# Conditional MLP with layer norm: fewer warm-up matmuls and a halved first cast at the start, the last batch's first tile's statistics on ScalarE at the end

## What is computed

```python
out_nr  = gelu(x @ w1_nr  + b1_nr)  @ w2_nr  + b2_nr
out_tsr = gelu(x @ w1_tsr + b1_tsr) @ w2_tsr + b2_tsr
h       = gelu(x @ w1_sr  + b1_sr)                      # 1024 wide
out_sr  = gelu(h @ w2_sr  + b2_sr)  @ w3_sr  + b3_sr
y   = x + where(c == 0, out_nr, where(c == 1, out_tsr, where(c == 2, out_sr, 0)))
mu  = mean(y); var = mean((y - mu) ** 2)                # over the 512 features
out = (y - mu) * rsqrt(var + 1e-5) * gamma + beta
```

## Time and profile before

| | us |
|---|---|
| median of 3 runs (lowest to highest) | 559.64 (559.57 to 559.65) |
| the profiled execution, its own time | 559.41 |
| span of the profiled execution, first to last instruction | 557.7 |
| TensorE busy | 549.6, 99% of the span |
| VectorE, ScalarE, GpSimd busy | 273.9, 213.5, 248.3 |

### The profile page before, as it was taken

The page is one execution under the profiler, slowest core; times in us unless marked ns, Lnnn a source line. Parts: engine busy times, 40 slices in busy tenths (PEclk is TensorE's granted clock), DMA queues, the critical chain, the costliest instruction groups (busy, mean ns, idle before and its releaser), DMA issues. The chain is left out here.

```text
span 557.7 us, 8222 instructions
## 1 busy us (share of the span) xinstructions
PE 549.6 (99%) x2423; PEld 453.4 (81%) x2424; DVE 273.9 (49%) x448; ACT 213.5 (38%) x328; POOL 248.3 (45%) x196
## 2 busy tenths in 40 slices
PE   9999999999999999999999999999999999999994
PEld 6888888888888888888888888888888888888883
DVE  5660176775856956114710569112765105601657
ACT  5451336145244354214421452424255124513351
POOL 0979898765674575300430046600174300430056
PEclk9999999999999999999999999999999999999998
DMA  8876405245344444200320044400244100410032
GB/s 313 339 237 190 152 7 196 100 151 188 109 155 145 156 150 141 84 0 0 138 87 0 1 158 142 150 0 0 75 150 159 66 0 29 154 43 0 0 135 91
DMA packets 26370, 61.28 MB, mean 110 GB/s; under 512 B 3058, under 2 KB 3314, under 8 KB 26226
## 3 DMA queue, kind: packets, MB, share of 16 engines
q1 hardware_dynamic: 26208, 60.97, 31.9%
q10 hardware_dynamic: 146, 0.13, 0.1%
HBM read 44.31 MB, written 16.78 MB: 110 GB/s over the span
## 5 line engine op out<-in xcount | busy, mean ns | idle before, releaser
L467 DVE TENSOR_TENSOR g_lo<-bank,g_hi 128x512 fp32r<-128x512 f32 x112 | 77.5, 692 | 251.0 <-DVEq L117 250.9
L415 ACT ACTIVATE g_hi<-bank,bcol 128x512 fp32r<-128x512 f32 x112 | 77.9, 695 | 165.9 <-ACTq L117 164.7
L620 POOL TENSOR_TENSOR rstd<-var_eps,power 128x2 f32<-128x2 f32 x30 | 21.0, 699 | 239.7 <-POOLq L117 239.7
L616 POOL TENSOR_TENSOR y<-y,row 128x512 f32<-128x512 f32 x64 | 95.7, 1514 | 49.1 <-POOLq L117 48.9
L437 ACT ACTIVATE y<-y,rstd 128x512 f32<-128x512 f32 x63 | 42.3, 717 | 166.3 <-ACTq L117 166.3
L244 PE MATMUL bank<-w_hi,g_hi 128*128 128x512 f32 x256 | 99.6, 389 | 0.0
L245 PE MATMUL bank<-w_lo,g_hi 128*128 128x512 f32 x256 | 99.6, 389 | 0.0
L246 PE MATMUL bank<-w_hi,g_lo 128*128 128x512 f32 x256 | 99.6, 389 | 0.0
L244 PE MATMUL bank<-x_hi,w_hi 128*128 128x512 f32 x240 | 93.4, 389 | 0.0
L245 PE MATMUL bank<-x_lo,w_hi 128*128 128x512 f32 x240 | 93.4, 389 | 0.0
L246 PE MATMUL bank<-x_hi,w_lo 128*128 128x512 f32 x240 | 93.4, 389 | 0.0
(11 more groups left out here) (42 smaller groups left out, 580.2 us busy)
## 6 DMA issues: line engine op xcount, KB each, us to landing
y<-x SPq DMA_DIRECT2D x64, 256.0 KB, 3.6
out<-y SPq DMA_DIRECT2D x63, 256.0 KB, 2.5
stage<-x_t SPq DMA_DIRECT2D x31, 512.0 KB, 3.3
w_raw<-weights SPq DMA_DIRECT2D x17, 512.0 KB, 5.1
row<-rows SPq DMA_DIRECT2D x1, 1280.0 KB, 11.0
stage<-x_t SPq DMA_DIRECT2D x2, 256.0 KB, 3.2
w_raw<-weights SPq DMA_DIRECT2D x2, 256.0 KB, 4.0
out<-y SPq DMA_DIRECT2D x1, 128.0 KB, 1.9
```

The costliest lines, as they stand in the source:

```text
L415: eng.activation(g_hi[:, slot, :], psum, ACT.Gelu, bias=b)
L467: eng.tensor_tensor(g_lo[:, slot, :], psum, g_hi32[:, slot, :], ALU.subtract).then_inc(s_gs, 1)
L616: eng.tensor_tensor(y[:, t, :], y[:, t, :], row[:, kind, :], ALU.add).then_inc(s_xb, 1)
L620: eng.tensor_tensor(rstd[:, t:t + n], var_eps[:, t:t + n], power[:, t:t + n], ALU.pow).then_inc(s_rstd, n)
```

## The change

At the start, 7 short matmuls on the constant are issued in place of 14. VectorE casts `w_hi` of chunks 0 and 1 in two halves of 256 columns, each raising `s_first_w`, and TensorE waits for the first half before `j` = 0 and for the second before `j` = 2. GpSimd sets one more small tile, `eps`.

In all batches but the last, epsilon is added for tiles 0 and 1 by GpSimd, inside `deviations(0, 2)`, and no longer by VectorE; for tiles 2 and 3 VectorE still does it.

In the last batch, ScalarE makes the statistics of tile 0, behind its last gelu: a copy of bank 4 with the sum of each row (`total`), the mean with minus sign, the mean into `mv`, the sum of squares of the deviations (`squares`), and the variance with epsilon. VectorE drops `bn_stats`, `bn_aggr` and `variance` of tile 0, waits for ScalarE before `centre` of tile 0, and does `variance` of tile 1 before `residual` of tile 2.

```diff
--- before.py
+++ after.py
@@ -38,7 +38,7 @@
 FINISHED_BY_OTHERS_END = TT - 1
 
 
-N_WARM, N_WARM_SHORT = 9, 14
+N_WARM, N_WARM_SHORT = 9, 7
 
 
 def conditional_mlp(nc, x, x_t, cond, weights, bias_cols, rows, out):
@@ -73,6 +73,8 @@
         rstd = sb("rstd", [P, TT])
         power = sb("power", [P, TT])
         unused = sb("unused", [1, 1])
+
+        total, minus_mean, squares, eps = sb("total", [P, 1]), sb("minus_mean", [P, 1]), sb("squares", [P, 1]), sb("eps", [P, 1])
         bank = [ctx.enter_context(nc.psum_tensor(f"bank{i}", [P, 512], fp32)) for i in range(8)]
 
         g_hi32 = g_hi[:, :, :].bitcast(fp32)
@@ -104,9 +106,11 @@
         s_y, s_acc = sem("s_y"), sem("s_acc")
         s_row = [sem(f"s_x_row{t}") for t in range(TT)]
         s_xb, s_ev, s_bn, s_mv = sem("s_xb"), sem("s_ev"), sem("s_bn"), sem("s_mv")
-        s_var = sem("s_var")
+        s_moments, s_eps, s_var = sem("s_moments"), sem("s_eps"), sem("s_var")
         s_own = sem("s_own")
         s_rstd, s_rstd_end = sem("s_rstd"), sem("s_rstd_end")
+        s_made, s_total, s_mean, s_squares, s_stats0, s_var0 = [
+            sem(n) for n in ("s_made", "s_total", "s_mean", "s_squares", "s_stats0", "s_var0")]
         s_v, s_v_end = sem("s_v"), sem("s_v_end")
         s_n = sem("s_n")
         s_fin, s_fin_end = sem("s_fin"), [sem(f"s_fin_end{h}") for h in range(2)]
@@ -287,7 +291,6 @@
                     take(eng, s_x01, 1)
                     for c in range(2):
                         eng.wait_ge(s_first, c + 1)
-                        eng.wait_ge(s_first_w, c + 1)
                         for which in range(3):
                             if which == 1:
                                 if c == 0:
@@ -298,6 +301,8 @@
                             if which == 2:
                                 eng.wait_ge(s_nr, 2 + c)
                             for j in range(HC):
+                                if which == 0 and j % 2 == 0:
+                                    eng.wait_ge(s_first_w, 2 * c + j // 2 + 1)
                                 part(j, c, which)
                         if c == 0:
                             read_next()
@@ -419,6 +424,20 @@
                 take(eng, s_full[f], 16)
                 eng.copy(x_hi[:, 2 * f:2 * f + 2, :], stage[:, f, :, :]).then_inc(s_hi, 1)
 
+            def first_tile_statistics(kind):
+
+                made = y[:, 0, :] if kind == NONE else bank[4][:, :]
+                take(eng, s_made)
+                eng.activation(bank[0][:, :], made, ACT.Copy, accum_out=total[:, :]).then_inc(s_total, 1)
+                take(eng, s_total)
+                eng.activation(minus_mean[:, :], total[:, :], ACT.Copy, scale=-1.0 / H).then_inc(s_mean, 1)
+                eng.activation(mv[:, 0, 0:1], total[:, :], ACT.Copy, scale=1.0 / H)
+                take(eng, s_mean)
+                eng.activation(bank[0][:, :], made, ACT.Square, bias=minus_mean[:, :], accum_out=squares[:, :]).then_inc(s_squares, 1)
+                take(eng, s_squares)
+                eng.sem_inc(s_stats0, 1)
+                eng.activation(var_eps[:, 0:1], squares[:, :], ACT.Identity, scale=1.0 / H, bias=eps[:, :]).then_inc(s_var0, 1)
+
             def body(kind, read_next, last):
                 for j in range(n_hidden(kind)):
                     gelu(bank[hidden_bank(kind, j)][:, :], j % 4, B1[kind] + j)
@@ -426,7 +445,9 @@
                 if kind == SR:
                     for i in range(HC):
                         gelu(bank[i][:, :], i, B2[SR] + i, (1, 1, 2, 0)[i])
-                if not last:
+                if last:
+                    first_tile_statistics(kind)
+                else:
                     split_x(0)
                     split_x(1)
                 for t in range(FINISHED_BY_OTHERS_END if last else TT):
@@ -475,11 +496,13 @@
             def made_in(kind, t):
                 return y[:, t, :] if kind == NONE else bank[4 + t][:, :]
 
-            def residual(kind, t):
+            def residual(kind, t, done=s_ev):
                 take(eng, s_xb)
                 if kind != NONE:
                     take(eng, s_y)
-                    eng.tensor_tensor(bank[4 + t][:, :], bank[4 + t][:, :], y[:, t, :], ALU.add).then_inc(s_ev, 1)
+                    eng.tensor_tensor(bank[4 + t][:, :], bank[4 + t][:, :], y[:, t, :], ALU.add).then_inc(done, 1)
+                elif done is s_made:
+                    eng.sem_inc(s_made, 1)
 
             def stats(kind, t):
                 if kind != NONE:
@@ -525,22 +548,24 @@
                     stats(kind, t + 1)
                     moments(kind, t)
                     moments(kind, t + 1)
-                    variance(t, 2)
+                    if t == 0:
+                        take(eng, s_mv, 2)
+                        eng.sem_inc(s_moments, 2)
+                    else:
+                        variance(t, 2)
                     centre(kind, t)
                     centre(kind, t + 1)
 
             def body_end(kind, read_next):
                 hidden(kind)
-                residual(kind, 0)
-                stats(kind, 0)
+                residual(kind, 0, s_made)
                 residual(kind, 1)
-                moments(kind, 0)
                 stats(kind, 1)
-                variance(0)
+                take(eng, s_stats0)
                 centre(kind, 0)
                 moments(kind, 1)
+                variance(1)
                 residual(kind, 2)
-                variance(1)
                 centre(kind, 1)
                 stats(kind, 2)
                 moments(kind, 2)
@@ -567,9 +592,10 @@
 
             for c in range(2):
                 eng.wait_ge(s_w_piece[c], 16)
-                eng.tensor_copy(w_hi[:, c, :], w_raw[:, c, :]).then_inc(s_first_w, 1)
+                for half in (slice(0, H // 2), slice(H // 2, H)):
+                    eng.tensor_copy(w_hi[:, c, half], w_raw[:, c, half]).then_inc(s_first_w, 1)
                 x_low(c, c + 1, (s_nr, s_x01)[c])
-                eng.wait_ge(s_first_w, c + 1)
+                eng.wait_ge(s_first_w, 2 * c + 2)
                 w_low(c, 0)
             x_low(2, 3, s_nr)
             x_low(3, 4, s_x23)
@@ -616,11 +642,17 @@
                         eng.tensor_tensor(y[:, t, :], y[:, t, :], row[:, kind, :], ALU.add).then_inc(s_xb, 1)
 
             def deviations(t, n):
-                take(eng, s_var, n)
+
+                if t == 0:
+                    take(eng, s_moments, n)
+                    eng.tensor_scalar(var_eps[:, t:t + n], mv[:, t:t + n, 1], EPS, None, ALU.add).then_inc(s_eps, n)
+                    take(eng, s_eps, n)
+                else:
+                    take(eng, s_var, n)
                 eng.tensor_tensor(rstd[:, t:t + n], var_eps[:, t:t + n], power[:, t:t + n], ALU.pow).then_inc(s_rstd, n)
 
-            def deviation_end(t, done=s_rstd):
-                take(eng, s_var)
+            def deviation_end(t, done=s_rstd, ready=s_var):
+                take(eng, ready)
                 eng.tensor_tensor(rstd[:, t:t + 1], var_eps[:, t:t + 1], power[:, t:t + 1], ALU.pow).then_inc(done, 1)
 
             def shift(t):
@@ -642,6 +674,7 @@
             def bias_end(kind, read_next):
                 add_bias(kind)
 
+            eng.memset(eps[:, :], EPS)
             eng.memset(power[:, :], -0.5).then_inc(s_power, 1)
             eng.wait_ge(s_power, 1)
             split(POOL_FIRST[0])
@@ -716,7 +749,7 @@
             deviations_of_all()
             shift_all()
             batch(eng, cond_of, NBATCH - 1, bias_end)
-            deviation_end(0)
+            deviation_end(0, ready=s_var0)
             deviation_end(1)
             shift(0)
             deviation_end(2)
```

## The result

The changed kernel takes **560.43 us** (median of 20 runs, 560.14 to 560.99) against 559.64 us before (20 runs, 559.34 to 560.23): a ratio of 1.0013, 95% interval 1.0007 to 1.0019. It is 0.8 us slower where 0.4 us of gain was forecast. It lies outside the range given (558.85 to 559.7), though still within 0.2%.

What follows compares the result with a forecast made beforehand. TensorE, busy 549.6 of 557.7 us, was taken as the bound. From the profiled 559.41 us, head -0.38, middle 0 and tail -0.02 gave 559.01; the median lying 0.23 higher, 559.24 us was forecast, range 558.85 to 559.7.

Steps and rivals of the forecast that it cites:

- The middle: Between head and tail: supplies not tied to TensorE still come in time, so cost 0.
- one late supply at 44 us: Last split of the SR first layer, called the tightest supply: margin falls from 0.50 to 0.12 us, still enough.
- rival 4: Head: clock rises later because products replace warm-up matmuls; 1.85 us slower, 561.5 us; chance 0.05.
- The head: Start: seven fewer short matmuls let the first product go at 5.25, not 6.00; 0.38 us gained.
- The rise stays where it is: Head: assumed TensorE's clock rises at the same moment in both kernels, so only 0.38 of 0.75 us is won.
- rival 3: Head: clock rises earlier relative to the products, so the whole 0.75 us is won; 558.87 us; chance 0.05.
- The small operations of the first batch: GpSimd gains an addition of 0 to 0.70 us, absorbed by its pause; VectorE loses one of 1.14 us.
- The tail: After the last matmul: 0.06 us won by VectorE, less 0.04 for waiting on ScalarE; gain 0.02 us.
- Rival 1: Tail: ScalarE's chain is longer, through 0.20 us read-outs or slower semaphores; 559.44 or 559.64 us; chance 0.17.
- The read-outs: Tail: ScalarE writes out the row sum twice, between 0 and 0.20 us each, taken as 0.10.
- the variance moves into the pause: Tail, VectorE: tile 1's variance moves from behind tile 2's addition into the pause ahead of it; 0.06 us won.
- what I don't see: Whole kernel: unforeseen effects, split between faster and slower; chance 0.03.

Runs made afterwards that it cites:

- e7: Changed kernel with 512 KB less in the load phase's DMA queue (weights sr1 2 issued only after sr2 0 landed): 559.35 us.
- e16: Changed kernel with 64 never executed instructions ahead of TensorE's loop and, in the last batch, tile 2's addition again ahead of tile 1's variance: 559.33 us.
- e1: Kernel before with 7 short warm-up matmuls in place of 14, nothing else: 559.55 us, ratio 0.9994.
- b2: Kernel before, unchanged, profiled once more to see whether its early fetch repeats: 560.02 us, one run.
- e4: Kernel before with 7 short warm-up matmuls and 14 executed filler instructions behind the warm-up: 560.35 us, ratio 1.0008.
- e11: Changed kernel with 512 KB less queued in the load phase and, in the last batch, tile 2's addition again ahead of tile 1's variance: 559.36 us.
- e17: Changed kernel with 64 never executed instructions, the old order of tile 2's addition and tile 1's variance, and 512 KB less queued: 559.13 us, ratio 0.9989.
- e13: Changed kernel with 64 never executed filler instructions ahead of TensorE's loop over the batches: 559.50 us, ratio 0.9998.
- e14: Changed kernel with 128 never executed filler instructions ahead of TensorE's loop over the batches: 559.54 us, ratio 1.0000.
- e8: Changed kernel with 512 KB more in the DMA queue (weights sr1 3 issued one landing earlier): 560.55 us, ratio 1.0014.
- e10: Kernel before with seven executed filler instructions on TensorE between warm-up and first product: 560.72 us, ratio 1.0016.

## Why the prediction was wrong

**The middle, costed at 0: the step that failed.** "Looked between them only for supplies that must not come late" was right as a plan, but I looked at data alone: weights, splits, `g`. TensorE's own instructions are a supply too, and before's margin there was smaller than it seemed: its sequencer reaches the end of the first batch's code 3.83 us ahead of the array, of which it wants 1.86 us behind the branch, so a branch may take some 2.0 us (e7's took 2.03, with a pause of 0.05). The fetch and what follows it take 1.03 + 1.55 = 2.6 us. In before the fetch had started 2.6 us ahead of the branch; in after 1.0 us behind it, and the branch took 3.58 us. Cost: 1.60 us in the profile, against a forecast of 0 that had looked at one late supply at 44 us. (That margin, 0.50 us in the prediction, was not safe either: see the waits at 44 us above.) No rival named it; rival 4 ended on the right side by another mechanism (a late clock), which the trace excludes, since the loads are at their 188 ns from 6.3 us on. The Trainium skill has the rule that I missed ("Runtime: NRT & Kernel Launch", section "Instruction fetch mechanics"): prefetch is sequential, in blocks of 16 KiB, and a taken branch to a block that isn't there stalls until it is fetched. The traces agree: eight have the fetch behind the start of the branch (+0.46 to +1.14 us), and in all eleven traces where the branch took over 1 us it ends 1.54 to 1.57 us behind the fetch's end. As it stands the page calls the cost of crossing a block mostly hidden; here it isn't.

**The head: right, -0.34 for -0.38.** First product at 5.26 (5.25 forecast), the next starts 0.21, 0.43 and 0.41 us apart, then nine of 0.225 to 0.235, then 0.227. Its reason was weaker than its number. "The rise stays where it is" held in this pair of traces (6.23 and 6.27), not in general: over the 20 traces, all with the first warm-up matmul at 0.82 us, the granted clock rose between 3.4 us (e16) and 9.9 us (e1), 6.45 in b2. That is how the Trainium skill has it ("TensorE: Matmul & The Clock Gate", section "What's actually happening"): the rise isn't tied to the kernel's start. So rival 3's mechanism is real, and my argument against it, three timed runs within 0.08 us, was none. But an early rise doesn't bring its 0.75 us: where it came at 3.9 us (e4) the 13th product started at 8.15, only 0.25 earlier than in after, because the loads then stood still ahead of the first product (0.63 us, which starts at 5.28, 0.11 behind the end of the cast of `w_hi`) and ahead of the 13th (0.27 us). A late rise, rival 4's price, came in e1's profiled run: TensorE stood still from 5.3 to 7.0, where data was late, the clock rose at 9.9, six products ran some 0.43 us apart, and the run took 561.63 us. That it was late because products and not warm-up stood before it, as rival 4 has it, is not shown.

**The small operations of the first batch: as forecast.** VectorE's 1.14 us addition is gone, and GpSimd's own took 0.22 us, nearer the lower end of 0 to 0.70:

```profile
29.27 0.22 POOL L648 TENSOR_SCALAR var_eps<-mv 128x2 f32<-128x2 f32 x1
29.67 0.72 POOL L652 TENSOR_TENSOR rstd<-var_eps,power 128x2 f32<-128x2 f32 x1 [0.18 <-POOLq L121]
...
32.84 0.70 POOL L652 TENSOR_TENSOR rstd<-var_eps,power 128x2 f32<-128x2 f32 x1 [1.31 <-POOLq L121]
```

**The tail: +0.09 for -0.02, the mis-sized term.** Rival 1's mechanism, ScalarE's chain, was not it. From residual 0's start to the centring of tile 0 I forecast 3.08 us; it took 2.98 (544.95 to 547.93), and before 2.96. The read-outs are instructions of 0.19 us, at the upper bound, but each starts 0.09 before its own pass has ended, so they add 0.11 and 0.12 us, about the 0.10 that I took. (The Trainium skill says of VectorE that such an operation is two instructions, "VectorE: DVE Perf Modes", section "Two Vector instructions with no wait between them"; on ScalarE the trace shows the same.) The wrong term is "the variance moves into the pause": I let the addition on tile 2 start 0.06 us behind the variance of tile 1, and it starts 0.26 behind (548.91 to 549.17). VectorE's sequencer takes the addition's two waits, for `s_xb` and for `s_y`, only behind the variance, at 548.955 and 549.067, and the addition starts at 549.175: 0.11 us each. In before neither cost anything: the one for `s_xb` was taken while VectorE centred tile 0 (546.92), and the one for `s_y` (547.73) is what ended the pause. From centring to addition it is 1.25 us, not 1.04, and the pause had room for 1.12 (546.71 to 547.83). So the addition is 0.15 us late against the last matmul, and the variance no longer behind it gives 0.06 back: 0.09. With the old order the 0.09 us are gone (e11, e16, e17) and the new statistics on ScalarE neither gain nor cost.

**How wide.** The range took in everything but rival 4 and "what I don't see" at 0.03. The second was worth more. That the time stays within 0.2% of before held; its direction did not. Without the pause (e13, e14) the changed kernel takes 559.50 and 559.54 us: inside the range, though not faster than before (559.54). The head's 0.34 us then meet the tail's 0.09 and the waits at 38 and 44 us, which cost e13's trace some 0.25 us from product 97 to 337 (54.65 against 54.40).

**What stays open.** What decides when TensorE's fetch is asked for. Shown are the place of its code (64 or 128 instructions never executed) and instructions executed ahead of the products (7 fillers), each sufficient in one direction; excluded are unused semaphores, the start of the products, and the emptying of the DMA queue as the thing waited for. Why after has the late fetch with 7 and with 14 shorts, and why e7's gate moves it, isn't explained. Two traits any explanation has to meet: in the five traces like before's the fetch starts 0.11 to 0.18 us behind the start of the same wait of TensorE's sequencer, the last ahead of the branch (21.22 in before), so it seems tied to a point of the program; and in the eight traces whose fetch starts at 24.3 to 24.8 without e7's gate (after, e1 to e4, e8 to e10) queue 1 had started 8.45 to 8.58 MB by then, in the five like before's 7.21 to 7.35. Not tested is the kernel's own hint for this branch (`branch_hint(ahead)`, the `BRANCH_PREFETCH_HINT` at the start of the batch): it is executed at 4.42 us in before and 2.90 in after, and in neither does a fetch follow for over 16 us. No run moves it or leaves it out.

## What to carry to other kernels

Where a saturated TensorE crosses a taken branch, count its instructions as a supply: here seven instructions ahead of the first product moved a 16 KB fetch from 2.6 us ahead of the branch to 1.1 us behind it, and cost more than the edit at the head saved. When a small edit costs time and the array stands still on "issue", read the sequencer's branch and the instruction queue before looking at data, and try the same kernel with 64 instructions that are never executed in front. A small operation put into a pause ahead of another one's waits can cost those waits too, 0.11 us each on VectorE here.

## What I had not expected of the hardware

- A branch of 3.6 us: in after a fetch of 16 KB starts 1.0 us behind the branch, runs 1.03 us, and the branch ends 1.56 us behind that.
- Seven executed sequencer instructions at 3 us cost 1.0 us at 28 us (e10); with 64 never executed ones the changed kernel takes 0.9 us less by the medians and 0.8 by the ratios to before (e13 against after).
- The rise of TensorE's clock between 3.4 and 9.9 us after the span's start in kernels whose warm-up begins at the same 0.82 us.
- ScalarE's sum of rows is written out by an instruction of its own, 0.19 us, of which 0.11 to 0.12 shows.
- GpSimd's addition on 128 x 2 elements took 0.22 us, its power on the same 0.70.
